# Attention with a mixture of experts on one core: the shifts of two groups of keys in one round of four 32-row products, and the output projection behind the projection of q

## The chip, the cores and the metric

The kernel runs on one core of a Trainium2 chip. Its time is the device time in microseconds (us); where several runs are given it is their median. The engines are TensorE (PE in the trace, its weight loads PEld), VectorE (DVE), ScalarE (ACT), GpSimd (POOL) and SyncE (SP), which issues all the transfers of this kernel.

## The reference

What is computed, cut to what matters (8 sequences of 512 tokens, width 128, 16 heads of width 64, 8 experts of which each token takes 2):

```python
q, k, v = (einsum('bsd,hdk->bhsk', x, w) for w in (w_q, w_k, w_v))
weights = softmax(einsum('bhqk,bhmk->bhqm', q, k) / sqrt(64), axis=-1)
z = einsum('bhqm,bhmk->bhqk', weights, v)
x1 = layernorm(x + x + concat_heads(z) @ w_o)
top2 = softmax over the two largest of x1 @ gate_w, zero for the other experts
y = sum over experts e of top2[..., e] * (silu(x1 @ w1[e]) @ w2[e])
out = layernorm(x1 + y)
```

## The kernel before

**Stages.** A short preamble loads and splits the inputs. Then comes the attention, which this change touches, and then the experts. The attention is a loop over 64 pairs (8 pairs of heads for each of 8 sequences). In PE's program, `body(n, j)` is one pair, with `j = n % 2` as the index of the double buffers. Bodies 0 to 7 and 62 and 63 are written out, and bodies 8 to 61 run in a hardware loop of two. Every engine has its own `body`, and semaphores alone order them. Operands are split into a high and a low part, so that a product is three products (high by high and two cross terms).

**Scores.** The scores stand transposed, keys on partitions and queries along the row. They are made in four groups of 128 keys (`t`), two heads at a time. Heads 0 and 1 lie in rows 0 to 63 and 64 to 127 of `q_pair` and `k_pair`, so each product has 64 rows, and the two heads' products stand beside one another in the array: one round. A group takes three rounds of q by k, and a fourth round (`step == 3`) that adds the shift, which is minus the row maximum of an earlier, coarse product. This round multiplies a row of ones by `shift`, which holds one row for each head at partitions 0 and 64 and zeros elsewhere. Group `t` lies in PSUM banks 0 and 1 for even `t`, 2 and 3 for odd `t`. ACT then takes the exponential of both banks in one instruction of 1024 columns (`exps`, line 835). So `scores` of group `t` has to wait until the exponential of group `t - 2` has freed the banks.

**Coarse products and row maxima.** Between the groups PE makes the coarse products of the next pair, one round for each `t` (`coarse`, line 526), in banks 4 and 5 or 6 and 7. DVE reduces each to row maxima (line 984), `shift_rows` (line 533) transposes them on PE, DVE copies them to `max_row` (line 991), and SP's `load_shift` (line 290) moves them to `shift` for the next pair. The second coarse product also waits until `zT` of an earlier pair is made (line 1012), because bank 7 holds it.

**The rest of a body.** Behind the four groups PE runs `project_out` (line 468 to 470, three products for the pair three back), `project_q` and `project_k` (the same lines, three products each, two pairs ahead), `shift_rows`, `project_v` in every even body, `sum_probs` (line 587) and `times_v` (line 572). The lines that set waits around the change are

```python
# project_q: bank 0 is free when the third exponential of pair m - 2 is done
pe.wait_ge(s["exp_done"], TT * (m - 2) + 3)
# project_v writes banks 2 and 3; ACT copies them to v behind the products with the old v
act.wait_ge(s["vT_done"], m // 2 + 1)
wait(act, s["pv_done"], m)
```

The next body may write banks 2 and 3 only when that copy (line 825) is done. In `scores` the wait for it (`v_done`) stands in front of group 1 of every odd body. POOL adds the exponentials up (`add_probs`, line 383) and then makes `zT_lo` (line 388), which `zT` of the next pair waits for.

Of the kernel before, what the change touches and what calls it, by code (L numbers as in the profile page):

```python
# [34 lines left out]
def attention_moe_kernel(nc, x, w_q, w_k, w_v, w_o, gate_w, w1, w2, out):  # L35
    B, S, D = x.shape
    H, _, DK = w_q.shape
# [3 lines left out]
    TT = S // P  # L41
# [6 lines left out]
    DMA = 16  # L48
    BLOCK = 32
    assert D == P and 2 * DK == P and S == 512 and HP == B and F == 2 * P  # L50

    with ExitStack() as ctx:
# [34 lines left out]
        shift = sb("shift", [P, 2, S], F32R)  # L87
# [94 lines left out]
        def wait(eng, semaphore, value):  # L182

            if not isinstance(value, int) or value > 0:
                eng.wait_ge(semaphore, value)
# [9 lines left out]
        def bits(ap):  # L195
            return ap.bitcast(F32)
# [49 lines left out]
        def is_last(n, ahead):  # L246
            return isinstance(n, int) and n + ahead >= PAIRS
# [9 lines left out]
        @block.sync  # L257
        def _(sp):
            def load_x(b):
                sp.dma_start(x_tok[:, b * TT:(b + 1) * TT, :], x_dram[:, b * TT:(b + 1) * TT, :]  # L260
                             ).then_inc(s["x0_in" if b == 0 else "x_near_in" if b < B // 2 else "x_far_in"], DMA)

            def load_w(k):
                sp.dma_start(w_raw[:, k, :].rearrange("p (h k) -> p h k", h=H), w_dram[k]).then_inc(w_sem[k], DMA)


            load_x(0)
            load_w(0)
            load_w(1)
            for b in range(1, B // 2):  # L270
                load_x(b)

            def load_wqk(m, j):


                if not (isinstance(m, int) and m < 4):
                    wait_apart(sp, (s["k_done"], m - 1))
                sp.dma_start(bits(wqk_cur[j][:]), bits(w_tab[:, m % HP, 0:2])).then_inc(wqk_cur_in[j], DMA)

            def load_xT(m):  # L280


                wait_apart(sp, (s["vT_done"], m // 2))
                sp.dma_start(bits(xT_cur[:]), bits(xT[:, m // HP])).then_inc(s["xT_cur_in"], DMA)

            def load_shift(m, j):


                wait_apart(sp, (s["max_row_done"], m + 1), (s["scores_done"], TT * (m - 1)))
                sp.dma_start(bits(shift[0:DK + 1:DK, j, :]), bits(max_row[:])).then_inc(s["shift_in"], DMA)  # L290


            load_w(2)
            sp.dma_start(w_raw[:, 3, :].rearrange("p (c d) -> p c d", c=HP),
                         w_o.rearrange("(c p) d -> p c d", p=P)).then_inc(w_sem[3], DMA)
            for b in range(B // 2, B):
                load_x(b)
            sp.dma_start(gate_raw[:], gate_w).then_inc(s["gate_in"], DMA)
            sp.wait_ge(s["w_split"], 2)
            load_wqk(2, 0)  # L300
            sp.wait_ge(s["xT_hi_done"], 1)
            sp.wait_ge(s["xT_lo_done"], 1)
            load_xT(0)
            load_shift(0, 0)

            def load_wo(m):

                wait_apart(sp, (s["wo_done"], m))
                sp.dma_start(bits(wo_cur[:]), bits(w_tab[:, m % HP, 3])).then_inc(s["wo_cur_in"], DMA)

            def body(n, j):
                if isinstance(n, int) and n == 1:

                    sp.wait_ge(s["w_split"], 4)
                    sp.wait_ge(s["xT_hi_done"], B)
                    sp.wait_ge(s["xT_lo_done"], B)
                    sp.dma_start(w1_raw, w1_dram).then_inc(s["experts_in"], DMA)
                if isinstance(n, int) and n == SPLIT_AT[2]:

                    sp.wait_ge(s["experts_split"], 2)  # L320
                    sp.dma_start(w2_raw, w2_dram).then_inc(s["experts_in"], DMA)
                if not is_last(n, 3):
                    load_wqk(n + 3, 1 - j)
                if j == 1 and not is_last(n, 1):
                    load_xT(n + 1)
                if not is_last(n, 1):
                    load_shift(n + 1, 1 - j)
                if exists(n, 2):
                    load_wo(n - 2)

            loops(sp, body)

            def load_accT(b):

                wait_apart(sp, (s["tok_done"], b))
                sp.dma_start(accT_cur[:], acc[:, b, :]).then_inc(s["accT_in"], DMA)

            def store(b):
                wait_apart(sp, (s["norm2_done"], TT * (b + 1)))
                sp.dma_start(out_dram[:, bass.ds(b * TT, TT), :], out_tok).then_inc(s["x_out"], DMA)  # L340


            sp.wait_ge(s["pv_done"], PAIRS - 1)
            sp.wait_ge(s["added"], (TT - 1) * (PAIRS - 1))
            load_accT(0)
            load_wo(PAIRS - 2)
            load_accT(1)
            load_wo(PAIRS - 1)
            sp.wait_ge(s["acc_done"], PAIRS)

            def chunk(b, j):
                if not past(b, 2):
                    load_accT(b + 2)
                if not is_first(b):
                    store(b - 1)

            chunks(sp, chunk)
            store(B - 1)
            sp.wait_ge(s["x_out"], DMA * B)
# [96 lines left out]
        def _(pe):  # L456
# [20 lines left out]
            def project_q(m, i, j):  # L477

                if isinstance(m, int) and m < 2:
                    pe.wait_ge(s["w_split"], 1)  # L480

                    wait(pe, s["q_lo_done"], m)
                else:
                    pe.wait_ge(wqk_cur_in[j], DMA * i)

                    pe.wait_ge(s["exp_done"], TT * (m - 2) + 3)
                project_qk(0, q_bank(m), m, j).then_inc(s["q_done"], 1)
# [45 lines left out]
                nc.tensor.transpose(psum[0:2 * TT, COARSE, 0:P], bits(neg_max[:].rearrange("p h t -> p (h t)")),  # L533
                                    ident[:]).then_inc(s["maxT_done"], 1)

            def scores(n, j, t, steps):

                keys = slice(t * P, (t + 1) * P)
                if steps[0] == 0:

                    wait(pe, s["exp_done"], TT * n + t - 1)
                    if t == 0:

                        pe.wait_ge(s["q_lo_done"], n + 2 if not is_last(n, 1) else PAIRS)
                        pe.wait_ge(s["k_lo_done"], n + 2 if not is_last(n, 1) else PAIRS)
                        if is_first(n):

                            pe.wait_ge(s["xT_lo_done"], B)
                    if t == 1 and j == 1:

                        pe.wait_ge(s["v_done"], (n - 1) // 2 + 1)
                for step in steps:
                    if step == 3 and t == 0:
                        pe.wait_ge(s["shift_in"], DMA * (n + 1))
                    for h in range(2):
                        rows = slice(h * DK, (h + 1) * DK)
                        left, right = ((k_pair[j][rows, 0, keys], q_pair[j][rows, 0, :]),
                                       (k_pair[j][rows, 1, keys], q_pair[j][rows, 0, :]),
                                       (k_pair[j][rows, 0, keys], q_pair[j][rows, 1, :]),
                                       (ones_row[rows, :], shift[rows, j, :]))[step]  # L560
                        mm = nc.tensor.matmul(psum[:, 2 * (t % 2) + h, :], left, right, start=(step == 0), stop=(step == 3))  # L561
                if steps[-1] == 3:
                    mm.then_inc(s["scores_done"], 1)

            def times_v(n, j, c):

# [58 lines left out]
            def body(n, j):  # L625
                ahead = not is_last(n, 1)

                def next_coarse(t):
                    if ahead:
                        coarse(n + 1, 1 - j, t)  # L630

                for t in range(TT):
                    next_coarse(t)
                    scores(n, j, t, (0, 1, 2, 3))
                if exists(n, 3):
                    project_out(n - 3)
                if not is_last(n, 2):
                    project_q(n + 2, (n + 2 - j) // 2, j)
                    project_k(n + 2, j)
                if ahead:  # L640
                    shift_rows(n + 1)
                if j == 0:
                    project_v(n)
                if exists(n, 1):
                    sum_probs(n - 1, 1 - j)
                    for c in range(TT):
                        times_v(n - 1, 1 - j, c)
# [310 lines left out]
        def _(dve):  # L958
# [28 lines left out]
            def shift_part(m):  # L987
                dve.wait_ge(s["maxT_done"], m + 1)

                wait(dve, s["shift_in"], DMA * m)  # L990
                nc.vector.tensor_copy(max_row[:], psum[0:2 * TT, COARSE, 0:P]).then_inc(s["max_row_done"], 1)

            def reciprocals(n):
# [262 lines left out]
```

## Time and profile before

| what | value |
|---|---|
| median of 3 runs (lowest, highest) | 1133.4 us (1131.9, 1135.74) |
| the profiled execution, its time | 1131.35 us |
| its span, first to last instruction | 1129.6 us |
| mean granted TensorE clock | 0.976 of full speed |
| PE, DVE, POOL, ACT busy | 93%, 70%, 64%, 52% of the span |

A busy PE is one whose pipeline holds a product, so small waits between two rounds don't show as idle time. A round's cost is read from the start of one product to the start of the next. The trace gives an instruction's start and duration in us, and in brackets how long its engine sat idle before it and what ended that.

### The profile page before, as it was taken

The numbers are of one execution on the slowest core, as the hardware profiler recorded it, in microseconds if no ns is written. First come the engines' busy times: TensorE is split into PE (matmuls) and PEld (weight loads), VectorE is DVE, ScalarE is ACT, GpSimd is POOL, SyncE is SP. The second block draws the span as 40 slices with busy tenths as digits, with TensorE's granted clock in tenths as the row PEclk, the third lists the DMA queues.
The fourth block names the chain that finished last, engine by engine and source line by source line (L and its number), as shares of the span: only waits on it lengthen the run. The fifth ranks groups of instructions, "written<-read, shape, count | busy, mean of one in ns | idle before, by whom it ended". The sixth has DMA issues, their size and how long they took to land. (4 is left out here: it accounts for less than half of the span.)

```text
span 1129.6 us, 19064 instructions
## 1 busy us (share of the span) xinstructions
PE 1054.5 (93%) x5912; PEld 668.8 (59%) x5912; DVE 792.4 (70%) x1172; ACT 583.2 (52%) x680; POOL 723.3 (64%) x372
## 2 busy tenths in 40 slices
PE   5999999999999999999999999999976988889886
PEld 3655556556665665566656655666545766667664
DVE  6777877767776777677767776776656677776774
ACT  4645455545554555455545554555426555566553
POOL 0687656776676567756765677567654665565665
PEclk8999999999999999999999999999998899999998
DMA  8221111111112111111121111111100000000000
GB/s 186 76 98 67 45 50 47 47 61 47 47 47 79 47 47 47 61 47 47 47 79 47 47 47 61 47 47 47 43 33 10 10 19 20 1 19 19 10 9 19
DMA packets 42106, 52.77 MB, mean 47 GB/s; under 512 B 9440, under 2 KB 28384, under 8 KB 42080
## 3 DMA queue, kind: packets, MB, share of 16 engines
q1 hardware_dynamic: 42080, 52.45, 13.4%
q8 instruction: 14, 0.23, 0.1%
q14 instruction: 12, 0.10, 0.0%
HBM read 6.30 MB, written 2.10 MB: 7 GB/s over the span
## 5 line engine op out<-in xcount | busy, mean ns | idle before, releaser
L984 DVE TENSOR_REDUCE neg_max<-psum 128x2 fp32r<-128x1024 f32 x256 | 295.8, 1217 | 3.9 <-PE psum L526 3.6
L561 PE MATMUL psum<-q_pair,k_pair 64*128 64x512 f32 x1536 | 226.2, 395 | 1.8 <-DVE xT L966 1.0
L835 ACT ACTIVATE probs_even<-psum 128x1024 f32<-128x1024 f32 x128 | 131.4, 1027 | 172.2 <-PE psum L561 164.0
L416 POOL TENSOR_TENSOR w_tab<-x_tok,w_tab 128x1024 fp32r<-128x1024 f32 x64 | 152.1, 2387 | 91.0 <-ACT w_tab L926 91.0
L561 PEld LDWEIGHTS psum<-q_pair,k_pair 64*128 64x128 f32 x1536 | 145.4, 186 | 34.1 <-ACT x_tok L835 11.1
L383 POOL TENSOR_TENSOR probs_sum<-x_tok 128x1024 f32<-128x1024 f32 x32 | 76.8, 2399 | 137.3 <-ACT x_tok L835 137.3
L383 POOL TENSOR_TENSOR probs_sum<-probs_even 128x1024 f32<-128x1024 f32 x32 | 76.7, 2396 | 134.9 <-ACT probs_even L835 134.9
L383 POOL TENSOR_TENSOR probs_sum<-probs_sum,probs_even 128x1024 f32<-128x1024 f32 x64 | 152.9, 2389 | 5.7
L383 POOL TENSOR_TENSOR probs_sum<-probs_sum,x_tok 128x1024 f32<-128x1024 f32 x64 | 151.9, 2373 | 5.7
L835 ACT ACTIVATE x_tok<-psum 128x1024 f32<-128x1024 f32 x128 | 131.1, 1026 | 24.8 <-PE psum L561 13.4
L1171 DVE TENSOR_TENSOR x_tok<-x_tok,psum 128x1024 f32<-128x1024 f32 x64 | 77.9, 1217 | 77.2 <-PE psum L709 47.7
L526 PE MATMUL psum<-k_pair,q_pair 64*128 64x512 f32 x512 | 114.7, 432 | 6.5 <-issue 2.0
L1012 DVE TENSOR_TENSOR zT<-psum,rec 128x512 f32<-128x512 f32 x64 | 44.3, 692 | 108.3 <-POOL zT_lo L388 58.2
L572 PE MATMUL psum<-x_tok,v 128*64 128x512 f32 x512 | 115.3, 592 | 0.0
L572 PE MATMUL psum<-probs_even,v 128*64 128x512 f32 x512 | 115.3, 592 | 0.0
L825 ACT ACTIVATE v<-psum 128x1024 f32<-128x1024 f32 x32 | 32.8, 1026 | 153.2 <-PE psum L572 152.3
L561 PE MATMUL psum<-shift,ones_row 64*128 64x512 f32 x512 | 104.4, 392 | 0.0
L526 PEld LDWEIGHTS psum<-k_pair,q_pair 64*128 64x128 f32 x512 | 49.8, 185 | 79.3 <-issue 68.4
L919 ACT ACTIVATE x_tok<-psum 128x1024 f32<-128x1024 f32 x64 | 65.5, 1025 | 57.5 <-PE psum L470 57.4
L572 PEld LDWEIGHTS psum<-x_tok,v 128*64 128x64 f32 x512 | 37.0, 137 | 72.9 <-issue 72.9
L572 PEld LDWEIGHTS psum<-probs_even,v 128*64 128x64 f32 x512 | 36.8, 137 | 73.1 <-issue 73.1
L388 POOL TENSOR_TENSOR zT_lo<-zT,zT_hi 128x512 fp32r<-128x512 f32 x62 | 78.8, 1271 | 0.0
(116 smaller groups left out, 1900.2 us busy)
## 6 DMA issues: line engine op xcount, KB each, us to landing
xT_cur<-xT SPq DMA_DIRECT2D x32, 512.0 KB, 2.9
wqk_cur<-w_tab SPq DMA_DIRECT2D x63, 256.0 KB, 2.3
wo_cur<-w_tab SPq DMA_DIRECT2D x64, 128.0 KB, 2.0
x_tok<-L_attn_x_dram SPq DMA_DIRECT2D x8, 256.0 KB, 5.2
probs_even<-acc SPq DMA_DIRECT2D x8, 256.0 KB, 2.3
out_dram<-probs_even SPq DMA_DIRECT2D x8, 256.0 KB, 2.3
shift<-max_row SPq DMA_DIRECT2D x64, 4.0 KB
acc<-L_ffn_w_dram SPq DMA_DIRECT2D x1, 1024.0 KB, 6.3
```

What stands on the lines that cost most here:

```text
L383: nc.gpsimd.tensor_tensor(probs_sum[j][:], left, probs[j][:, :, c, :], ALU.add).then_inc(s["added"], 1)
L388: nc.gpsimd.tensor_tensor(zT_lo[:], zT[:], bits(zT_hi[:]), ALU.subtract).then_inc(s["zT_lo_done"], 1)
L416: nc.gpsimd.tensor_tensor(g_lo[e % GB], gated[e % 2], bits(g_hi[e % GB]), ALU.subtract).then_inc(s["g_lo_done"], 1)
L526: mm = nc.tensor.matmul(psum[:, coarse_bank(t) + h, :], q_pair[j][rows, 0, t * P:(t + 1) * P], k_pair[j][rows, 0, :], start=True, stop=True)
L561: mm = nc.tensor.matmul(psum[:, 2 * (t % 2) + h, :], left, right, start=(step == 0), stop=(step == 3))
L572: mm = nc.tensor.matmul(psum[h * DK:(h + 1) * DK, Z, :], v[:, j, c, h, :], probs[j][:, h, c, :], start=(c == 0), stop=(c == TT - 1))
L825: nc.scalar.activation(v[:].rearrange("p j t h k -> p t j (h k)"), psum[:, 2:4, :].rearrange("p b (t j k) -> p (b t) j k", t=2, j=2), ACT. ...
L835: nc.scalar.activation(probs[j][:, :, t, :], psum[:, 2 * (t % 2):2 * (t % 2) + 2, :], ACT.Exp).then_inc(s["exp_done"], 1)
L919: nc.scalar.activation(silu[e % 2], psum[:, FC * (e % 2):FC * (e % 2 + 1), :], ACT.Silu).then_inc(s["silu_done"], 1)
L984: nc.vector.tensor_reduce(neg_max[:, :, t:t + 1], psum[:, coarse_bank(t):coarse_bank(t) + 2, :], AX.X, ALU.max, negate=True).then_inc(s["m ...
L1012: nc.vector.tensor_tensor(zT[:], psum[:, Z, :], rec[:], ALU.mult).then_inc(s["z_done"], 1)
L1171: nc.vector.tensor_tensor(gated[e % 2], silu[e % 2], psum[:, CB, :].unsqueeze(1).broadcast_to([P, FC, S]), ALU.mult).then_inc(s["gated"], 1)
```

## The change

`scores` loses its fourth round. A new function, `shifts(n, j, t)`, stands for two groups at once. It makes four products of 32 rows each, two heads by the groups `t` and `t + 1`, in four banks. For this `shift` has its rows twice, at partitions 0 and 64 and again at 32 and 96, and so SP issues two transfers in place of one. The even group is opened by its q by k products and closed by `shifts`. The odd group is opened by `shifts` and closed by its q by k products. `shifts` waits for the exponential that last used the odd group's banks, and the wait for `v_done` moves to it, from in front of group 1 to the end of group 0. The order of PE's work in a body becomes: coarse 0, group 0, shifts of 0 and 1, coarse 1, group 1, group 2, coarse 2, shifts of 2 and 3, group 3, coarse 3. `project_q` now stands in front of `project_out`.

```diff
 wait_apart(sp, (s["max_row_done"], m + 1), (s["scores_done"], TT * (m - 1)))
-sp.dma_start(bits(shift[0:DK + 1:DK, j, :]), bits(max_row[:])).then_inc(s["shift_in"], DMA)
+for copy in range(2):
+    sp.dma_start(bits(shift[copy * BLOCK:copy * BLOCK + DK + 1:DK, j, :]), bits(max_row[:])).then_inc(s["shift_in"], DMA)
...
-def scores(n, j, t, steps):
+def scores(n, j, t):
     keys = slice(t * P, (t + 1) * P)
-    if steps[0] == 0:
+    if t % 2 == 0:
         wait(pe, s["exp_done"], TT * n + t - 1)
...
-        if t == 1 and j == 1:
-            pe.wait_ge(s["v_done"], (n - 1) // 2 + 1)
-    for step in steps:
-        if step == 3 and t == 0:
-            pe.wait_ge(s["shift_in"], DMA * (n + 1))
+    for step in range(3):
         for h in range(2):
...
-            mm = nc.tensor.matmul(psum[:, 2 * (t % 2) + h, :], left, right, start=(step == 0), stop=(step == 3))
-    if steps[-1] == 3:
+            mm = nc.tensor.matmul(psum[:, 2 * (t % 2) + h, :], left, right, start=(t % 2 == 0 and step == 0),
+                                  stop=(t % 2 == 1 and step == 2))
+    if t % 2 == 1:
         mm.then_inc(s["scores_done"], 1)
+
+def shifts(n, j, t):
+    wait(pe, s["exp_done"], TT * n + t)
+    if t == 0:
+        pe.wait_ge(s["shift_in"], 2 * DMA * (n + 1))
+        if j == 1:
+            pe.wait_ge(s["v_done"], (n - 1) // 2 + 1)
+    for u in (1, 0):
+        for h in range(2):
+            rows = slice(h * DK + u * BLOCK, h * DK + (u + 1) * BLOCK)
+            mm = nc.tensor.matmul(psum[:, 2 * u + h, :], ones_row[rows, :], shift[rows, j, :],
+                                  start=(u == 1), stop=(u == 0))
+    mm.then_inc(s["scores_done"], 1)
...
-for t in range(TT):
-    next_coarse(t)
-    scores(n, j, t, (0, 1, 2, 3))
+next_coarse(0)
+scores(n, j, 0)
+shifts(n, j, 0)
+next_coarse(1)
+scores(n, j, 1)
+scores(n, j, 2)
+next_coarse(2)
+shifts(n, j, 2)
+scores(n, j, 3)
+next_coarse(3)
+if not is_last(n, 2):
+    project_q(n + 2, (n + 2 - j) // 2, j)
 if exists(n, 3):
     project_out(n - 3)
 if not is_last(n, 2):
-    project_q(n + 2, (n + 2 - j) // 2, j)
     project_k(n + 2, j)
...
-wait(dve, s["shift_in"], DMA * m)
+wait(dve, s["shift_in"], 2 * DMA * m)
```

## Rows read from the trace of the kernel before

**Rows 1.** Head of the page: span; busy us, share of the span, instructions.

```profile
span 1129.6 us, 19064 instructions
PE 1054.5 (93%) x5912; PEld 668.8 (59%) x5912; DVE 792.4 (70%) x1172; ACT 583.2 (52%) x680; POOL 723.3 (64%) x372
```

**Rows 2.** Windows, mid-loop: length; PE, PEld, DVE, ACT, POOL busy; clock; DMA share, GB/s.

```profile
200.00:300.00 100.00, 99.80 (x610) 59.30 (x608) 71.80 (x97) 50.31 (x61) 66.78 (x33) 1.00 0.14 53
```

**Rows 3.** Timeline, PE: first coarse products of bodies 10 and 60 (start, us, instruction).

```profile
153.38 0.50 PE L526 MATMUL psum<-k_pair,q_pair 64*128 64x512 f32 x2
...
780.61 0.49 PE L526 MATMUL psum<-k_pair,q_pair 64*128 64x512 f32 x2
```

**Rows 4.** Timeline, PE, body 38 (even).

```profile
504.64 0.50 PE L526 MATMUL psum<-k_pair,q_pair 64*128 64x512 f32 x2
...
505.68 0.40 PE L561 MATMUL psum<-shift,ones_row 64*128 64x512 f32 x2
506.12 0.50 PE L526 MATMUL psum<-k_pair,q_pair 64*128 64x512 f32 x2
...
511.99 0.27 PE L533 MATMUL psum<-ident,neg_max 128*8 128x128 f32 x1
```

**Rows 5.** Timeline, PE, body 39 (odd), and the start of body 40.

```profile
518.05 0.50 PE L526 MATMUL psum<-k_pair,q_pair 64*128 64x512 f32 x2
518.38 0.86 PE L561 MATMUL psum<-q_pair,k_pair 64*128 64x512 f32 x6
519.08 0.39 PE L561 MATMUL psum<-shift,ones_row 64*128 64x512 f32 x2
519.31 0.40 PE L526 MATMUL psum<-k_pair,q_pair 64*128 64x512 f32 x2
...
520.70 0.63 PE L561 MATMUL psum<-q_pair,k_pair 64*128 64x512 f32 x4
...
522.54 0.41 PE L561 MATMUL psum<-shift,ones_row 64*128 64x512 f32 x2
522.88 0.50 PE L468 MATMUL psum<-zT_hi,wo_cur 128*128 128x512 f32 x1
...
523.69 0.40 PE L468 MATMUL psum<-xT,wqk_cur 128*128 x1
...
525.08 0.27 PE L533 MATMUL psum<-ident,neg_max 128*8 128x128 f32 x1
...
529.73 0.50 PE L526 MATMUL psum<-k_pair,q_pair 64*128 64x512 f32 x2
```

**Rows 6.** Timeline, ACT: first exponential of body 38; v copy, first exponential of 39.

```profile
506.11 1.03 ACT L835 ACTIVATE probs_even<-psum 128x1024 f32<-128x1024 f32 x1 [4.80 <-PE psum L561]
...
518.23 1.02 ACT L825 ACTIVATE v<-psum 128x1024 f32<-128x1024 f32 x1 [4.92 <-PE psum L572]
519.51 1.02 ACT L835 ACTIVATE x_tok<-psum 128x1024 f32<-128x1024 f32 x1 [0.26 <-PE psum L561]
```

**Rows 7.** Timeline, weight loads that had waited: body 38 (first row), 39 (the others).

```profile
509.78 0.19 PEld L468 LDWEIGHTS psum<-zT_hi,wo_cur 128*128 128x128 f32 x1 [0.37 <-DVE neg_max L984]
...
519.37 0.37 PEld L561 LDWEIGHTS psum<-q_pair,k_pair 64*128 64x128 f32 x4
...
520.59 0.54 PEld L561 LDWEIGHTS psum<-q_pair,k_pair 64*128 64x128 f32 x6 [0.16 <-ACT x_tok L835]
```

**Rows 8.** Timeline, DVE: third maxima of body 38, zT in body 40.

```profile
508.20 1.22 DVE L984 TENSOR_REDUCE neg_max<-psum 128x2 fp32r<-128x1024 f32 x1
...
530.41 0.69 DVE L1012 TENSOR_TENSOR zT<-psum,rec 128x512 f32<-128x512 f32 x1 [1.79 <-POOL zT_lo L388]
```

**Rows 9.** Timeline, POOL, around the start of body 40.

```profile
529.04 1.27 POOL L388 TENSOR_TENSOR zT_lo<-zT,zT_hi 128x512 fp32r<-128x512 f32 x1
```

**Rows 10.** Timeline, SP: the shift's transfer issued in body 39.

```profile
525.93 0.59 SPq L290 DMA_DIRECT2D shift<-max_row  x1
```

**Rows 11.** Page, transfers issued: tile, queue, operation, count, KB each, us to landing.

```profile
wo_cur<-w_tab SPq DMA_DIRECT2D x64, 128.0 KB, 2.0
```

More of the change, by code:

```diff
@@ L558, in scores @@
                                        (k_pair[j][rows, 1, keys], q_pair[j][rows, 0, :]),
-                                       (k_pair[j][rows, 0, keys], q_pair[j][rows, 1, :]),
-                                       (ones_row[rows, :], shift[rows, j, :]))[step]
-                        mm = nc.tensor.matmul(psum[:, 2 * (t % 2) + h, :], left, right, start=(step == 0), stop=(step == 3))
-                if steps[-1] == 3:
+                                       (k_pair[j][rows, 0, keys], q_pair[j][rows, 1, :]))[step]
+                        mm = nc.tensor.matmul(psum[:, 2 * (t % 2) + h, :], left, right, start=(t % 2 == 0 and step == 0),
+                                              stop=(t % 2 == 1 and step == 2))
+                if t % 2 == 1:
                     mm.then_inc(s["scores_done"], 1)
+            def shifts(n, j, t):
[10 more added lines that the diff above has]
+                mm.then_inc(s["scores_done"], 1)
             def times_v(n, j, c):
```

## The prediction

> **What bounds the kernel now.** I read the page first: a span of 1129.6 us in which TensorE (PE) is busy for 93%, the next engine for 70% [rows 1]. Then the windows by stage. In the middle of the attention PE is busy 99.80 of 100 us at a granted clock of 1.00 [rows 2], so no idle time is in sight. But a busy PE hides small waits, so I went to the timeline and measured from the start of one round to the start of the next. The loop repeats exactly: the first coarse products of bodies 10 and 60 lie 627.23 us apart, 25 times 25.09 [rows 3]. Body 38 takes 13.41 us and body 39 11.68 [rows 4, 5], and what holds for these two holds 27 times.
>
> Inside body 39 three rounds take 0.70 us (518.38 to 519.08), so a round is 0.23 [rows 5]. An exponential lasts 1.03 and starts 0.43 behind the start of the round that closes its group (519.08 to 519.51) [rows 5, 6]. The weights of group 2 are loaded 0.06 after the end of exponential 0 (520.53 to 520.59), and that load is marked as held by the exponential; its product starts at 520.70, 0.17 after the exponential's end [rows 5 to 7]. So from a closing round to the first round that may reuse its banks there are 0.43 + 1.02 + 0.17 = 1.62 us, seven rounds. Seven rounds (coarse 1, four of group 1, coarse 2 and the closing one itself) lie there now. The score phase of an odd body is thus bound by PE and by the exponentials alike, with nearly no slack. The even body loses 0.2 elsewhere: its second coarse product starts 1.48 behind the first in place of 1.26 [rows 4, 5], because zT ends late [rows 8].
>
> **The change part by part.** *Two rounds fewer in each body.* If four 32-row products cost one round, as two 64-row products do now (two products, 0.39 us together [rows 5]), this removes 2 x 0.23 = 0.46 us of PE a body. The rows show no 32-row product. The price lies between one round and two (0.46); I take one, since the h = 0 and h = 1 products already run beside one another. The Trainium skill, page "TensorE: Matmul & The Clock Gate", Part 3, gives four row tiles a measured speedup of 3.07, not 4. By that a call would cost some 0.07 more, and the sum below about 8 us more, as an estimate.
>
> *A change of tile shape twice in each call.* Where PE goes from 64-row to 128-row products, the next load starts 0.34 after the last round's start, and the product's longer row (0.50 against 0.40) puts its real start at 522.99, 0.45 behind the round before, with nothing to wait for in odd bodies [rows 5]. A change of shape thus loses 0.45 - 0.23 = 0.22. Each `shifts` goes from 64 rows to 32 and back: four changes a body. Whether this one costs the same no row shows, so it lies between 0 and 0.22; I take 0.22, the only price on record. With 0.22 the sum below is 46.0 us, with 0 it is 33.0. The Trainium skill holds for any pair of shapes what the rows show for one, and so stands for the 46.0 (page "TensorEngine Tiling (Array Packing)", Tiling Modes, Key Properties: changing the tiling mode drains the array).
>
> *The order of waits.* Between the closing round of group 0 and the first round of group 2 there are now five rounds (shifts, coarse 1, three of group 1), where the exponential needs seven. In front of `project_q`, which needs the third exponential, stand shifts 2, three rounds of group 3 and coarse 3: again five, where `project_out` gave three more. That is where the stall goes. I step through an even body, in us from its first coarse product:
> - shifts 0: 1.03, plus 0.22, at 1.25. Exponential 0 from 1.68 to 2.71.
> - coarse 1 at 1.70 (a round and a change), group 1 from 1.93 to 2.39; its exponential from 2.82 to 3.85.
> - group 2 would start at 2.62, but waits for 2.71 + 0.17 = 2.88. Coarse 2 at 3.57.
> - shifts 2 at 4.02 (round and change), and exponential 1 + 0.17 gives 4.02 too. Exponential 2 from 4.45 to 5.48.
> - group 3 from 4.47, coarse 3 at 5.16; `project_q` could start at 5.61, but waits for exponential 2. From that end to its load I take 0.20: the held load of group 2 came 0.06 behind its releaser [rows 7], while a 128-row load waiting on DVE came 0.36 behind its own (508.20 + 1.22 to 509.78) [rows 7, 8], and `project_q` has an address to work out first, so I choose the middle. Load to product is 0.11 (the 0.50 row against 0.39). `project_q` at 5.79.
> - nine rounds of projections: `project_q` to `shift_rows` with six took 1.39, and three more 0.70 [rows 5], so `shift_rows` at 7.88. Before: 511.99 - 504.64 = 7.35 [rows 4]. **Even body: +0.53.**
>
> *The wait for `v_done`.* ACT copies v at the very start of an odd body, from 518.23 to 519.25, 1.20 behind the body's start [rows 6]. The first load behind that wait came at 519.37, 0.12 later, and was just covered by coarse 1 [rows 7]. Now the cover is gone: the wait stands in front of shifts 0, whose turn is at 1.25, and it can start at 1.20 + 0.12 + 0.11 = 1.43. Group 1, coarse 1 and all of ACT's exponentials queue behind it. The same steps: exponential 0 from 1.86 to 2.89, group 2 at 3.06, shifts 2 at 4.20, exponential 2 from 4.63 to 5.66, `project_q` at 5.97, `shift_rows` at 8.06. Before: 525.08 - 518.05 = 7.03 [rows 5]. **Odd body: +1.03.**
>
> *What costs nothing.* The second transfer of the shift: its issue takes 0.59 of SP [rows 10]. It was issued 7.88 after the body's start and needed 4.8 later. Now the second is issued at about 9.5 and done being issued at 10.1; with the 2.0 us of a 128 KB transfer as its landing [rows 11] it is there at 12.1, and the next body's shifts come at 13.9. If that cover were gone, PE would stall by what is missing. `load_wo` and `load_wqk` behind it on SP move by 0.6 and have a body's time. `project_out` in second place: its wait, the third maxima, ends near 5.2, before it starts at 6.5. Late maxima (coarse 3 at 5.16, so done near 6.8) end before `shift_rows`. The wait of even bodies for zT goes: POOL starts 0.3 to 0.4 later in the odd body, zT ends at 531.10 + 0.4, and body 40 starts 1.03 later, so zT is there 0.7 after that start, when coarse 1 is due at 1.70 [rows 5, 8, 9]. This gain is already in the even body's steps.
>
> *The sum.* Two bodies: 0.53 + 1.03 = 1.56; 27 x 1.56 = 42.1. The other ten bodies have other waits of start-up and end, and I count them at half, 10 x 0.39 = 3.9. Together 46.0. On the profiled execution: 1131.35 + 46.0 = 1177.4. The median of the runs is 2.05 higher, so **1179 us**.
>
> **The rivals.**
> 1. *The four products don't run side by side*, but two and then two. Then the call ends 0.23 later, exponential 0 and 2 each start that much later, and `project_q` comes 0.46 later: 59 bodies x 0.46 = 27, 1206 us. For it: no 32-row row exists. Against it: 64-row products do share a round. Chance 0.10.
> 2. *Faster: the freed rounds count in full.* Place: the first round of group 2 and `project_q`. The point from which it decides: if banks were free again within five rounds (1.14 us) of the closing round in place of 1.62, nothing would wait there. The price is then 62 x 0.46 = 28.5 off, and the 0.22 of the even bodies (27 x 0.22 = 5.9): 1133.4 - 34.4 = 1099. For it: PE is the busiest engine. Against it: an exponential alone takes 1.02, and the held load shows that even seven rounds just suffice. Chance 0.07.
> 3. *No change*: the waits come to just what the rounds save. They would have to be 0.46 a body, plus half of 0.22; the least that I can make of them is more (below). Chance 0.03.
>
> **How the numbers follow.** The main case, the exponential's round trip laid bare, has 0.80. Its own range: without the cost of shape changes 13 less, with `project_q`'s load at 0.06 another 0.14 x 59 = 8 less (1158); at 0.36 another 9 more (1188). Rival 1 is centred on 1206, and I take in about half of it. Below 1158 I leave room for waits that a row before doesn't show. Range 1148 to 1206. A measurement of this kernel tells from no change what is over 0.3%, some 3.4 us. Slower by more: the main case and rival 1, 0.90. Within: 0.03. Faster: 0.07.
>
> **What would show it.** In the changed trace: group 2's load in every body marked as held by an exponential; `project_q`'s first load likewise; shifts 0 of odd bodies held until v is copied, 1.4 behind the body's start; a gap of about 0.45 rather than 0.23 on either side of each 32-row round; four 32-row products starting within some hundredths of one another; `shift_rows` near 7.9 and 8.1; two bodies near 26.6 us. Wrong would be: bodies of 24.2 us (rival 2); products that start 0.2 apart in two couples (rival 1); or a stall at `shift_in`, which I count as covered.

## The result and the profile after

The changed kernel takes 1181.99 us (median of 4 runs, 1179.66 to 1184.15), where the kernel before takes 1134.52 in the four runs beside it. The ratio is 1.0421, 95% interval [1.0392, 1.045]: slower by 47 us. 1179 was forecast, with a range of 1148 to 1206.

The head of the page of the changed kernel, and its windows in the middle of the attention (columns as in [rows 1, 2]):

```profile
span 1177.9 us, 19132 instructions
PE 1089.9 (93%) x5912; PEld 632.7 (54%) x5912; DVE 806.4 (68%) x1172; ACT 576.2 (49%) x680; POOL 722.8 (61%) x372
...
200.00:300.00 100.00, 98.11 (x573) 52.06 (x572) 69.69 (x90) 48.04 (x58) 63.07 (x30) 1.00 0.12 44
```

PE has as many products as before and still looks nearly full, 98.11 of 100 us at a clock of 1.00. But 573 products ran in this stretch where 610 ran before [rows 2]. The busy share doesn't show the loss, the count does. The span is 48.3 us longer.

The timeline of PE, bodies 38 (even) and 39 (odd), against [rows 4, 5]; the line numbers have moved (L527 coarse, L556 scores, L572 `shifts`, L534 `shift_rows`):

```profile
532.20 0.50 PE L527 MATMUL psum<-k_pair,q_pair 64*128 64x512 f32 x2
532.53 0.87 PE L556 MATMUL psum<-q_pair,k_pair 64*128 64x512 f32 x6
533.33 0.50 PE L572 MATMUL psum<-shift,ones_row 32*128 32x512 f32 x4
533.76 0.50 PE L527 MATMUL psum<-k_pair,q_pair 64*128 64x512 f32 x2
...
537.33 0.40 PE L527 MATMUL psum<-k_pair,q_pair 64*128 64x512 f32 x2
537.86 0.49 PE L469 MATMUL psum<-xT,wqk_cur 128*128 x1
...
540.05 0.27 PE L534 MATMUL psum<-ident,neg_max 128*8 128x128 f32 x1
...
546.11 0.50 PE L527 MATMUL psum<-k_pair,q_pair 64*128 64x512 f32 x2
546.45 0.86 PE L556 MATMUL psum<-q_pair,k_pair 64*128 64x512 f32 x6
547.46 0.51 PE L572 MATMUL psum<-shift,ones_row 32*128 32x512 f32 x4 [0.15 <-ACT v L844]
...
552.09 0.49 PE L469 MATMUL psum<-xT,wqk_cur 128*128 x1 [0.23 <-ACT x_tok L854]
...
554.29 0.27 PE L534 MATMUL psum<-ident,neg_max 128*8 128x128 f32 x1
...
558.94 0.50 PE L527 MATMUL psum<-k_pair,q_pair 64*128 64x512 f32 x2
```

The four 32-row products do run beside one another: one row of four, 0.50 us long. `shift_rows` comes 7.85 behind the start of the even body (7.35 before) and 8.18 behind that of the odd one (7.03 before). Two bodies take 26.74 us in place of 25.09. In odd bodies the call is held by the copy of v, and `project_q` by the third exponential.

The weight loads of the same bodies that had waited (even body first), and the exponentials of the even body:

```profile
533.33 0.19 PEld L572 LDWEIGHTS psum<-shift,ones_row 32*128 32x128 f32 x4 [0.37 <-issue]
533.76 0.19 PEld L527 LDWEIGHTS psum<-k_pair,q_pair 64*128 64x128 f32 x2 [0.24 <-issue]
534.96 0.53 PEld L556 LDWEIGHTS psum<-q_pair,k_pair 64*128 64x128 f32 x6 [0.43 <-ACT probs_even L854]
536.09 0.19 PEld L572 LDWEIGHTS psum<-shift,ones_row 32*128 32x128 f32 x4 [0.37 <-ACT probs_even L854]
537.85 0.19 PEld L469 LDWEIGHTS psum<-xT,wqk_cur 128*128 128x128 f32 x1 [0.56 <-issue]
...
549.09 0.53 PEld L556 LDWEIGHTS psum<-q_pair,k_pair 64*128 64x128 f32 x6 [0.43 <-ACT x_tok L854]
552.09 0.19 PEld L469 LDWEIGHTS psum<-xT,wqk_cur 128*128 128x128 f32 x1 [0.66 <-issue]
```

```profile
533.88 1.03 ACT L854 ACTIVATE probs_even<-psum 128x1024 f32<-128x1024 f32 x1 [5.02 <-PE psum L572]
535.01 1.03 ACT L854 ACTIVATE probs_even<-psum 128x1024 f32<-128x1024 f32 x1
536.64 1.94 ACT L854 ACTIVATE probs_even<-psum 128x1024 f32<-128x1024 f32 x2 [0.60 <-PE psum L572]
```

Exponential 0 ends at 534.91, and the load of group 2 follows at 534.96, held by it. The bracket of `shifts` of group 2 names exponential 1, which ends at 536.04, 0.05 before the load. But the load also comes 0.33 behind coarse 2 (535.76), which the change of tile shape takes by itself: with short exponentials it is 0.32 (below). So that wait adds 0.01 at most. ACT then idles for 0.60, and exponential 2 (536.64 to 537.67) holds `project_q`, whose load comes at 537.85. That load's bracket says "issue". Between the exponential's end and the load the trace has instructions of PE's sequencer, which these views leave out: one in the even body (537.7) and two in the odd body (551.84 and 551.95). In the odd body the product's own row names ACT.

### The profile page after: what moved, and what is told of

It reads as the page before. It is cut to its first block and busy times, and to the rows that moved or that the text cites. A ratio compares the mean times of both kernels' runs of the same rounds, so it can differ in the third digit from the quotient of the medians.

```text
span 1177.9 us, 19132 instructions
## 1 busy us (share of the span) xinstructions
PE 1089.9 (93%) x5912; PEld 632.7 (54%) x5912; DVE 806.4 (68%) x1172; ACT 576.2 (49%) x680; POOL 722.8 (61%) x372
## 5 line engine op out<-in xcount | busy, mean ns | idle before, releaser
L1003 DVE TENSOR_REDUCE neg_max<-psum 128x2 fp32r<-128x1024 f32 x256 | 312.8, 1224 | 78.6 <-PE psum L527 77.7
L556 PE MATMUL psum<-q_pair,k_pair 64*128 64x512 f32 x1536 | 234.3, 411 | 1.9 <-DVE xT L985 1.0
L854 ACT ACTIVATE probs_even<-psum 128x1024 f32<-128x1024 f32 x128 | 127.7, 1024 | 180.6 <-PE psum L572 176.7
L556 PEld LDWEIGHTS psum<-q_pair,k_pair 64*128 64x128 f32 x1536 | 136.0, 186 | 62.6 <-issue 18.3
L854 ACT ACTIVATE x_tok<-psum 128x1024 f32<-128x1024 f32 x128 | 127.4, 1023 | 44.7 <-PE psum L572 40.9
L527 PE MATMUL psum<-k_pair,q_pair 64*128 64x512 f32 x512 | 115.4, 447 | 3.8 <-DVE k_pair L995 1.4
L938 ACT ACTIVATE x_tok<-psum 128x1024 f32<-128x1024 f32 x64 | 65.5, 1025 | 58.0 <-PE psum L471 57.9
L527 PEld LDWEIGHTS psum<-k_pair,q_pair 64*128 64x128 f32 x512 | 48.2, 184 | 76.4 <-issue 68.7
L1047 DVE TENSOR_TENSOR acc<-psum,acc 128x512 f32 (+1 forms) x64 | 44.3, 692 | 56.7 <-PE psum L471 56.7
```

The source lines that it names most:

```text
L527: mm = nc.tensor.matmul(psum[:, coarse_bank(t) + h, :], q_pair[j][rows, 0, t * P:(t + 1) * P], k_pair[j][rows, 0, :], start=True, stop=True)
L854: nc.scalar.activation(probs[j][:, :, t, :], psum[:, 2 * (t % 2):2 * (t % 2) + 2, :], ACT.Exp).then_inc(s["exp_done"], 1)
L938: nc.scalar.activation(silu[e % 2], psum[:, FC * (e % 2):FC * (e % 2 + 1), :], ACT.Silu).then_inc(s["silu_done"], 1)
L1003: nc.vector.tensor_reduce(neg_max[:, :, t:t + 1], psum[:, coarse_bank(t):coarse_bank(t) + 2, :], AX.X, ALU.max, negate=True).then_inc(s["m ...
L1047: nc.vector.tensor_tensor(a, psum[:, out_bank(n), :], a, ALU.add).then_inc(s["acc_done"], 1)
```

## The experiments

Times are medians; each ratio is to the kernel before on the same chip, with its 95% interval.

**64 rows again, the closing round second.** The joint call stays; only the tile shape and the saved rounds are undone.

```diff
-rows = slice(h * DK + u * BLOCK, h * DK + (u + 1) * BLOCK)
+rows = slice(h * DK, (h + 1) * DK)
```

> The changed kernel with 64-row products in `shifts` again: four products in two rounds, same place, same order, same waits (ones at the partitions of the second copy of the shift are zero). It takes the changes of tile shape away and gives the saved rounds back. Theory A (the exponential's round trip is laid bare by joining two groups in one call, and the changes of shape mostly stand inside those waits): the round that closes the even group now comes second, so exponential 2 starts 0.16 later in even bodies and 0.35 later in odd ones, and the time rises by about 15 us, to 1197. Theory B (the changes of shape are the loss): four changes of 0.22 go and two rounds of 0.23 come back, 0.42 us a body off, about 1155.

Measured: 1192.55 us, 1.0521 [1.0487, 1.0554]. It is slower than the change by some 11 us, so theory B's 1155 falls. With 32 rows the joint call is cheaper than with 64. The sign is right and the size is somewhat less than the 15 expected. But the run doesn't clear the changes of shape. PE, body 38:

```profile
536.94 0.50 PE L531 MATMUL psum<-k_pair,q_pair 64*128 64x512 f32 x2
...
537.98 0.62 PE L576 MATMUL psum<-shift,ones_row 64*128 64x512 f32 x4
...
540.51 0.40 PE L531 MATMUL psum<-k_pair,q_pair 64*128 64x512 f32 x2
540.75 0.62 PE L576 MATMUL psum<-shift,ones_row 64*128 64x512 f32 x4
```

The closing round stands second in each call, a round of 0.23 behind the call's start: at 1.27 and 4.04. In the change the one round starts at 1.24 and 4.00, behind a change of shape. The edit thus put a round where a change of shape had been, at about the same price. By the trace's mean over the loop, even bodies are 0.05 longer than in the change and odd ones 0.25: there the change of shape passes while PE waits for v, and a round behind that wait doesn't.

**64 rows, the closing round first and without waits.**

```diff
+for u in (0, 1):
+    if u == 1:
+        wait(pe, s["exp_done"], TT * n + t)
+        if t == 0 and j == 1:
+            pe.wait_ge(s["v_done"], (n - 1) // 2 + 1)
     for h in range(2):
...
+    if u == 0:
+        mm.then_inc(s["scores_done"], 1)
```

> As the first, with 64-row products, but the round that closes the even group comes first and does not wait; the waits for the exponential of the odd banks and for v stand between the two rounds. So the joint wait is undone, and the order of groups, coarse products and projections stays that of the change. Theory A: exponential 2 no longer waits for exponential 1, exponential 0 of odd bodies no longer for v; `shift_rows` comes near 7.4 and 7.5 after the body's start, 1.09 less for two bodies, so about 1150. Theory C (the new order of groups and projections is the loss, whatever the round): stays within 5 us of 1182.

Measured: 1150.22 us, 1.0154 [1.0127, 1.0182], the number of theory A. The only difference to the experiment before is which of the two rounds stands first and where the two waits stand, and it is worth 42 us. PE in the even body of this run with the load of group 2, and PE in the odd body:

```profile
513.00 0.50 PE L531 MATMUL psum<-k_pair,q_pair 64*128 64x512 f32 x2
...
514.03 0.62 PE L576 MATMUL psum<-shift,ones_row 64*128 64x512 f32 x4
...
516.58 0.63 PE L576 MATMUL psum<-shift,ones_row 64*128 64x512 f32 x4
```

```profile
515.54 0.53 PEld L560 LDWEIGHTS psum<-q_pair,k_pair 64*128 64x128 f32 x6 [0.41 <-ACT probs_even L859]
```

```profile
526.49 0.50 PE L531 MATMUL psum<-k_pair,q_pair 64*128 64x512 f32 x2
526.83 0.86 PE L560 MATMUL psum<-q_pair,k_pair 64*128 64x512 f32 x6
527.52 0.81 PE L576 MATMUL psum<-shift,ones_row 64*128 64x512 f32 x4
```

In the odd body the first of the two shift rounds starts 1.03 behind the body's start again, where the joint call had to wait until 1.46. The 0.81 shows that the second round, which needs the banks of v, is the one that now waits.

The even body shows no wait for banks that was undone: in the experiment before, the second call followed coarse 2 by 0.24, a round. What it wins is the place of the closing rounds, which now start at 1.03 and 3.58 in place of 1.27 and 4.04. By the trace's means even bodies are 0.48 shorter than in the experiment before, two rounds, and odd ones 0.90, two rounds and some 0.4 of waiting for v. So the number came true, but the wait for exponential 1, one of theory A's reasons, had no part in it. Group 2 still waits for exponential 0: six rounds lie between, and its product (load at 515.54 and 0.11 more) starts 1.62 behind the closing round.

**The output projection in front again.**

```diff
-if not is_last(n, 2):
-    project_q(n + 2, (n + 2 - j) // 2, j)
 if exists(n, 3):
     project_out(n - 3)
 if not is_last(n, 2):
+    project_q(n + 2, (n + 2 - j) // 2, j)
     project_k(n + 2, j)
```

> The changed kernel with `project_out` in front of `project_q` again, nothing else. Theory A: the three rounds of the output projection cover the wait for exponential 2; 0.19 off in even and 0.29 off in odd bodies, about 1168. If the swap did nothing: 1182. If the swap were the whole loss: 1135.

Measured: 1169.16 us, 1.0323 [1.0296, 1.035]: 13 less than the change, as expected. PE, body 38:

```profile
524.07 0.50 PE L527 MATMUL psum<-k_pair,q_pair 64*128 64x512 f32 x2
...
529.19 0.40 PE L527 MATMUL psum<-k_pair,q_pair 64*128 64x512 f32 x2
529.52 0.50 PE L469 MATMUL psum<-zT_hi,wo_cur 128*128 128x512 f32 x1
...
531.72 0.27 PE L534 MATMUL psum<-ident,neg_max 128*8 128x128 f32 x1
```

The projection's load follows the last coarse round after 0.33, where `project_q`'s came after 0.53 in the change, and `shift_rows` comes at 7.65 in place of 7.85.

**The price of a change of tile shape.** The kernel before, with 32 rows in the fourth round:

```diff
-rows = slice(h * DK, (h + 1) * DK)
+rows = slice(h * DK, h * DK + (BLOCK if step == 3 else DK))
```

> The kernel before, where only the products of the fourth round have 32 rows in place of 64 (two of them, one for each head, rows 0 to 31 and 64 to 95); no round is saved, order and waits are unchanged. It prices the change of tile shape by itself: seven more changes a body. If each costs 0.22: 1.54 us a body, less about 0.2 of waits that were there in even bodies, some 90 us more, 1223. If 32 and 64 rows change without loss: 1134.

Measured: 1209.31 us, 1.0666 [1.0632, 1.0701]: slower by 77 us with the same work in the same order. PE, body 38 of this run:

```profile
551.08 0.50 PE L526 MATMUL psum<-k_pair,q_pair 64*128 64x512 f32 x2
551.41 0.86 PE L561 MATMUL psum<-q_pair,k_pair 64*128 64x512 f32 x6
552.20 0.49 PE L561 MATMUL psum<-shift,ones_row 32*128 32x512 f32 x2
552.63 0.50 PE L526 MATMUL psum<-k_pair,q_pair 64*128 64x512 f32 x2
...
554.20 0.50 PE L526 MATMUL psum<-k_pair,q_pair 64*128 64x512 f32 x2
```

From one coarse round to the next five rounds pass, 1.55 and 1.57 us, where five rounds of one shape take 1.15 (519.31 to 520.47 is 1.16 [rows 5], and that held a small wait). So a change costs 0.20, close to the 0.22 assumed. The 14 us by which the expectation was too high are mostly this difference: 63 bodies x 7 x 0.02 = 9.

**The wait for v.**

```diff
-if j == 1:
-    pe.wait_ge(s["v_done"], (n - 1) // 2 + 1)
+if isinstance(n, int) and n == 1:
+    pe.wait_ge(s["v_done"], 1)
...
-if j == 0:
+if is_first(n):
     v_part(n)
```

> The changed kernel that leaves out every copy of v past the first (all pairs use the v of the first two; the products of project_v still run), and with it the wait for v in front of `shifts` of group 0. It prices that wait. Theory A: shifts of odd bodies start at 1.24 behind the body's start, as in even bodies, in place of 1.46; 0.22 less in 31 bodies, some 7 us, 1175. If the wait for v is hidden by other waits: 1182. If it were the larger half of the loss: below 1160.

Measured: 1173.13 us, 1.0346 [1.0324, 1.0368]. The medians lie 9 us apart; 7 were expected. The trace gives the wait itself less: the call of an odd body starts at 1.23, `shift_rows` comes at 7.97 in place of 8.18, and 31 times 0.21 is 6.5. The rest is the spread of executions: one of this run's four took 1177.29, the others about 1173.

**The swap alone, in the kernel before.** The third experiment's diff, the other way round, on the kernel before.

> The kernel before with `project_q` in front of `project_out`, the change's last part alone. Theory A: `project_q` then waits for exponential 2 in this order too; it comes at 5.4 in even bodies and 5.2 in odd ones, 0.17 and 0.27 later than `project_out` does now: some 13 us more, 1146. If the swap costs only together with the joint call: 1133.

Measured: 1138.26 us, 1.0035 [1.0021, 1.0049]. The swap costs, but 5 us and not 13: a miss. PE, start of body 38 and of 39 with its end:

```profile
507.11 0.50 PE L526 MATMUL psum<-k_pair,q_pair 64*128 64x512 f32 x2
...
508.38 0.45 PE L526 MATMUL psum<-k_pair,q_pair 64*128 64x512 f32 x2
...
514.37 0.27 PE L533 MATMUL psum<-ident,neg_max 128*8 128x128 f32 x1
...
520.42 0.50 PE L526 MATMUL psum<-k_pair,q_pair 64*128 64x512 f32 x2
...
527.73 0.27 PE L533 MATMUL psum<-ident,neg_max 128*8 128x128 f32 x1
```

The odd body is later by what was expected (7.31 for 7.03, 0.28). But the even body is quicker than before, 7.26 for 7.35: its second coarse product comes at 1.27 in place of 1.48. A longer odd body gives POOL time to finish `zT_lo`, which ends 0.32 behind the start of body 38 in place of 0.58, and so pays back the wait for zT. The expectation had left this out, though the prediction had it. Against an even body without that wait (7.04, last experiment) the swap costs 0.22 here too.

**The second transfer alone, in the kernel before.**

```diff
-sp.dma_start(bits(shift[0:DK + 1:DK, j, :]), bits(max_row[:])).then_inc(s["shift_in"], DMA)
+for copy in range(2):
+    sp.dma_start(bits(shift[copy * BLOCK:copy * BLOCK + DK + 1:DK, j, :]), bits(max_row[:])).then_inc(s["shift_in"], DMA)
...
```

> The kernel before with the shift's transfer made twice, to partitions 0 and 64 and to 32 and 96 (ones at the partitions of the second copy are zero), products of 64 rows as before. It tests that the second transfer is covered: 1133, within 0.3%. If the queue of SP or the landing were late, PE would stand at the shift round, some tenths a body, 20 us or more.

Measured: 1131.54 us, 0.9982 [0.997, 0.9993]. The second transfer costs nothing, as counted.

**Short exponentials.** The changed kernel, and the kernel before with the same edit:

```diff
...
-nc.scalar.activation(probs[j][:, :, t, :], psum[:, 2 * (t % 2):2 * (t % 2) + 2, :],
-                     ACT.Exp).then_inc(s["exp_done"], 1)
+nc.scalar.activation(probs[j][:, 0, t, :], psum[:, 2 * (t % 2), :], ACT.Exp).then_inc(s["exp_done"], 1)
```

> The changed kernel with the exponentials of the first head of each pair alone (512 columns in place of 1024; the second head's are left out and a constant or old data stands in their place). It takes the exponential's round trip off PE's path, from 1.62 to about 1.2 us, and leaves rounds and changes of shape. Theory A: group 2 and `project_q` no longer wait; left are four changes of 0.21 less two rounds, and the wait for v in odd bodies: `shift_rows` at 7.39 and 7.61, some 30 us less, 1152. If the changes of shape were all: no change, 1182.

> The kernel before with the same exponentials left out, as the measure for the run above. Its rounds already cover the round trip, so only the small waits go (zT comes earlier too): about 12 us less, 1121. The difference to the run above is then the price of the change with short exponentials: by theory A changes of shape net of the rounds saved, 0.43 a body, and 0.22 in odd bodies for v, some 31 us. If the exponential's latency were the whole loss, the change would now be faster than this by up to 28 us.

Measured: 1148.38 us, 1.0131 [1.0105, 1.0157], and 1117.11 us, 0.9857 [0.9841, 0.9874]. An exponential now takes 0.60, and weight loads of the changed kernel, body 38, read:

```profile
514.72 0.19 PEld L574 LDWEIGHTS psum<-shift,ones_row 32*128 32x128 f32 x4 [0.37 <-issue]
...
515.26 1.35 PEld L558 LDWEIGHTS psum<-q_pair,k_pair 64*128 64x128 f32 x12
...
517.19 0.19 PEld L574 LDWEIGHTS psum<-shift,ones_row 32*128 32x128 f32 x4 [0.35 <-ACT probs_even L856]
```

The twelve loads of groups 1 and 2 run through without a wait. The last row's bracket names exponential 1, but that had ended at 516.99; the load comes 0.32 behind coarse 2 (516.87), a change of shape. `shift_rows` comes at 7.37 and 7.59, where 7.39 and 7.61 were expected. What is left between the two kernels is 31 us, as expected: two changes of shape around each call, less the rounds saved, and v. So some 16 of the 47 us go with the length of the exponentials, and even where PE no longer waits for them the change would lose here.

**What is left of the change.** The second experiment, and `project_out` in front as well:

> The second experiment (64-row rounds, the closing one first) with `project_out` in front of `project_q` as well. What is left of the change is the order of the groups and coarse products, and the second transfer. Theory A: 0.17 and 0.07 less than the second experiment, about 1143, some 10 above before. If the rest of the loss sat in the projections: 1133.

Measured: 1142.93 us, 1.0078 [1.006, 1.0096], as expected. The order of groups and coarse products, with the place of the wait for v that goes with it, is worth 10 us. It falls in odd bodies: by the trace's means `shift_rows` comes there at 7.45 in place of 7.03, and in even ones, which no longer wait for zT, at 7.27 in place of 7.35.

**A version quicker than both.** The kernel before, with `zT_lo` between POOL's second and third addition:

```diff
 add_probs(n, j):
     for c in range(1, TT):
...
+        if c == 2 and exists(n, 2):
+            zT_part(n - 2)
...
-if exists(n, 2):
-    zT_part(n - 2)
```

> Not part of the change: the kernel before, with POOL making `zT_lo` between its second and third addition of exponentials in place of behind them, 2.4 us earlier. It tests the wait for zT that even bodies had before and that the change lost. If that wait is POOL's lateness, the second coarse product of even bodies comes 1.26 behind the first in place of 1.48, the maxima start earlier too, and even bodies become as quick to `shift_rows` as odd ones, 7.03 for 7.35: some 9 us less, 1124. If something else holds zT, no change.

Measured: 1125.19 us, 0.9917 [0.9897, 0.9937]. POOL, before body 38 of this run, and PE in that body:

```profile
495.83 1.26 POOL L390 TENSOR_TENSOR zT_lo<-zT,zT_hi 128x512 fp32r<-128x512 f32 x1
```

```profile
498.94 0.49 PE L526 MATMUL psum<-k_pair,q_pair 64*128 64x512 f32 x2
...
500.20 0.40 PE L526 MATMUL psum<-k_pair,q_pair 64*128 64x512 f32 x2
...
505.98 0.27 PE L533 MATMUL psum<-ident,neg_max 128*8 128x128 f32 x1
```

`zT_lo` ends at 497.09, before the body starts, where it ended 0.58 behind a body's start before (530.31 against 529.73 [rows 5, 9]). The second coarse product comes at 1.26, and `shift_rows` at 7.04 in place of 7.35. This is the one real wait that the change removed, had without the change. In the changed kernel zT of body 38 is held by PE's product and no longer by POOL:

```profile
532.47 0.69 DVE L1031 TENSOR_TENSOR zT<-psum,rec 128x512 f32<-128x512 f32 x1 [1.39 <-PE psum L583]
```

## Why the prediction was right

Right in sign and size, and step by step in the mechanism; the likeliest case came true, and the rivals fell. One of its terms rests on a row that was read wrongly, and came out right by luck.

- *Two rounds fewer, four products in one round*: right, and so rival 1 falls. The first 32-row product of a call and the coarse product behind it lie 0.43 apart, a round and a change of shape, as with two such products in the round (552.20 to 552.63 in the run that priced the change of tile shape). So a speedup under 4 doesn't show here.
- *Changes of shape*: 0.22 was taken, 0.20 measured by the experiment made for it. The prediction stretched a price read between 64 and 128 rows to 64 and 32, and it held. Its steps say which of the four changes of a body count: the two in front of a closing round, while the two behind it pass in the exponential's round trip. The first experiment agrees, though it proves less than it seems to: it put a round in the place of each change that counts. The 33.0 without a price no run tests, since none has a 32-row round without a change of shape.
- *The exponential's round trip*: right step by step. The even body's group 2 was put at 2.88, and its product came 0.11 behind a load at 2.76, at 2.87; shifts 2 at 4.02, measured 4.00; `project_q` at 5.79, measured 5.77; `shift_rows` at 7.88, measured 7.85. Rival 2 needed banks to be free within five rounds, and every load of group 2 shown is held by an exponential.
- *The wait for v*: 1.43 was expected for shifts 0 of odd bodies; the row at 1.35 and 0.11 more give 1.46. Worth 6 to 7 us by the trace.
- *The odd body*: +1.03 was forecast, +1.15 measured. The term that was too small is the way from exponential 2 to `project_q`'s load: 0.20 was taken for both bodies, and it is 0.18 in the even body and 0.29 in the odd one (551.80 to 552.09; exponential 2 starts at 550.77 by the same timeline and lasts 1.03), where a second sequencer instruction stands in the way. The 0.20 was luck. It is the middle between 0.06 and a load that came 0.36 behind DVE; but that load came 0.33 behind PE's closing round (`509.45 0.40 PE L561 MATMUL psum<-shift,ones_row 64*128 64x512 f32 x2`, load at 509.78 [rows 7]). That is the change of shape from 64 to 128 rows, which the prediction itself priced at 0.34 from round to load where nothing was waited for.
- *What costs nothing*: the second transfer and the late row maxima were covered, as said; no row of `shifts` waits for a transfer.
- *The sum*: 27 x 1.65 = 44.6 in the loop, 42.1 forecast; the other ten bodies came to 48.3 - 44.6 = 3.7, with 3.9 counted at half rate. Behind the last `shift_rows` both profiled executions take 317.9 us, so the whole loss is in front of it.

Put one behind the other, the experiments give the loss as a chain: order of groups and second transfer, 1133 to 1143; `project_q` first, to 1150; the closing round second and the call's waits at its head, to 1193; 32 rows in place of 64, back to 1182. A step's size depends on what stands around it: the swap of the projections is worth 5 us in the kernel before, 7 in this chain and 13 in the change. And the last two steps belong together. Against 1150, where the closing round stands first, the change's call itself loses 32 us. In even bodies that is the change of shape in front of each closing round (1.24 in place of 1.03, and as much again at the second call); in odd bodies the first of the two passes in the wait for v (1.46 in place of 1.03). The wait for exponential 1, which the call also has at its head, costs 0.01 at most. What all steps share is that the exponential's round trip of 1.62 runs from the closing round: what stands in front of that round counts in full, and a round taken away behind it wins nothing while the round trip lasts longer. The prediction had no such split, since its steps hold all of this at once; that it came out near does not make each term its own cause.

## What to carry to other kernels

Count the rounds between the instruction that closes a group and the first one that needs its banks again, and compare with the consumer's whole round trip, before taking rounds out of that stretch: here seven rounds just covered 1.62 us, and six and five did not. A call that serves two buffers inherits the waits of both, so put the closing product, which can start at once, first. And two changes of tile shape (0.40) cost nearly as much as two rounds (0.46), so a packed round between rounds of another shape must save more than that.

## What the runs showed of the hardware

A change between 64-row and 32-row products costs PE 0.20 us in either direction, about as much as from 64 to 128 rows (0.22), and the four weight loads of a 32-row round start together and take 0.19 us, as one does. In the profile's loads such a change reads as 0.24 or 0.37 of "issue" with no releaser; where an exponential ended shortly before, the bracket names it although the load did not wait for it (517.19, short exponentials).
